# Fewer copies of the features in memory, reads cut in halves and in kinds, and attention's last period rearranged

## The reference, cut to what matters

```python
x = x + attn_a(layernorm(x), Wq, Wk, Wv, Wo)
x = x + ffn(layernorm(x), gate_cp, up_cp, down_cp)
x = x + attn_b(layernorm(x), Wq, Wk, Wog, Wig, g_weight)
x = x + ffn(layernorm(x), gate_cp, up_cp, down_cp)
```

## Time and profile before

| | us |
|---|---|
| median of 3 runs | 833.07 (832.21 to 833.85) |
| profiled execution, its own time | 834.41 |
| its span | 832.7 |
| PE busy | 772.9 (93%) |
| DVE busy | 625.8 (75%) |
| ACT busy | 493.9 (59%) |
| packets of SP's transfers | 108.47 MB, 49.3% of 16 engines |

### The profile page before, as it was taken

How to read it: one execution, slowest core, us unless ns; L and a number is a source line. 1 busy time by engine, 2 the same in 40 slices (tenths; PEclk the granted TensorE clock), 3 DMA queues, 4 the chain that set the end, 5 groups by cost and what they waited for, 6 DMA issues and landing times.

```text
span 832.7 us, 19301 instructions
## 1 busy us (share of the span) xinstructions
PE 772.9 (93%) x6818; PEld 661.5 (79%) x6818; DVE 625.8 (75%) x1269; ACT 493.9 (59%) x967; POOL 244.1 (29%) x321
## 2 busy tenths in 40 slices
PE   7789999999999999779999989999999879999988
PEld 7667777777777777559989878998888859988887
DVE  5677777777787788557887768689887667777765
ACT  3145555555554556565666656678887746666643
POOL 4056743222223233311100010166566470000000
PEclk9899999999999999869999999999999989999999
DMA  6765557666586456675666630000043135777731
GB/s 166 115 135 88 93 100 114 97 96 93 87 147 99 80 81 98 210 260 206 232 238 238 236 132 2 1 2 0 2 149 142 38 142 194 273 264 262 261 131 52
DMA packets 70983, 111.48 MB, mean 134 GB/s; under 512 B 7061, under 2 KB 27958, under 8 KB 70854
## 3 DMA queue, kind: packets, MB, share of 16 engines
q1 hardware_dynamic: 68848, 108.47, 49.3%
q10 hardware_dynamic: 2048, 1.88, 1.1%
HBM read 41.82 MB, written 42.81 MB: 102 GB/s over the span
## 4 chain that ended last, share of the span: by engine, by line
PE 54%; DVE 12%; DMA 10%; SPq 9%; issue 9%; ACT 6%; ACTq 0%; DVEq 0%; POOL 0%; POOLq 0%
PE bank L417 8%; PE bank L419 7%; PE bank L418 7%; DMA stk<-fx 5%; PE pair_a L923 5%; SPq L607 4%; PE bank L937 3%; PE pair_b L892 3%; DVE inter L1968 3%; DMA fx<-fs 2%; PE pair_a L1228 2%; SPq L490 2%; DVE spline L2046 2%; PE pair_a L1173 2%; ACT gact L1547 2%
## 5 line engine op out<-in xcount | busy, mean ns | idle before, releaser
L417 PE MATMUL bank<-wd_hi,in_hi 128*128 128x256 f32 x512 | 147.0, 287 | 0.9 <-DVE in_lo L1973 0.8
L419 PE MATMUL bank<-wd_hi,in_lo 128*128 128x256 f32 x512 | 146.1, 285 | 0.0
L418 PE MATMUL bank<-wd_lo,in_hi 128*128 128x256 f32 x512 | 145.9, 285 | 0.0
L1790 DVE TENSOR_REDUCE mx<-pair_b 128x6 f32<-128x768 f32 x124 | 117.9, 951 | 34.4 <-PE pair_b L904 32.2
L1555 ACT ACTIVATE in_hi<-inter 128x512 fp32r<-128x512 f32 x128 | 80.7, 631 | 105.6 <-DVE inter L1968 101.6
L683 POOL TENSOR_SCALAR_AFFINE_SELECT prob<-prob 128x512 f32<-128x512 f32 x128 | 82.1, 642 | 201.4 <-ACT prob L1390 201.3
L1390 ACT ACTIVATE prob<-pair_a 128x768 f32<-128x768 f32 x128 | 103.6, 810 | 63.0 <-PE pair_a L923 61.2
L1973 DVE TENSOR_TENSOR in_lo<-inter,in_hi 128x512 fp32r<-128x512 f32 x128 | 89.0, 695 | 60.9 <-ACT in_hi L1555 59.4
L417 PEld LDWEIGHTS bank<-wd_hi,in_hi 128*128 128x128 f32 x512 | 98.3, 192 | 6.2 <-DVE in_lo L1973 1.7
L418 PEld LDWEIGHTS bank<-wd_lo,in_hi 128*128 128x128 f32 x512 | 98.2, 192 | 4.8
L419 PEld LDWEIGHTS bank<-wd_hi,in_lo 128*128 128x128 f32 x512 | 98.1, 192 | 0.0
(11 more groups left out here) (233 smaller groups left out, 1960.3 us busy)
## 6 DMA issues: line engine op xcount, KB each, us to landing
stk<-fx SPq DMA_DIRECT2D x128, 252.0 KB
stack<-stage SPq DMA_DIRECT2D x184, 128.0 KB, 4.4
fx<-fs SPq DMA_DIRECT2D x32, 512.0 KB, 3.6
fx<-fs SPq DMA_DIRECT2D x32, 256.0 KB, 3.8
fx<-fs SPq DMA_DIRECT2D x16, 504.0 KB
fx<-fs SPq DMA_DIRECT2D x16, 252.0 KB
X<-in_attn_a_x SPq DMA_DIRECT2D x14, 256.0 KB, 5.4
result<-X SPq DMA_DIRECT2D x7, 512.0 KB, 8.0
```

The costliest lines, as they stand in the source:

```text
L417: pe.matmul(dst, l_hi, r_hi, start=first, stop=False)
L418: pe.matmul(dst, l_hi, r_lo, start=False, stop=False)
L419: return pe.matmul(dst, l_lo, r_hi, start=False, stop=last)
L1790: dve.tensor_reduce(mx[:, h, :, p % PR, :], src[:, :, 0:3 * P].rearrange("p n (t k) -> p n t k", t=3), AX.X, ALU.max).then_inc(a_mx, 1)
```

## The change

Fewer copies: `fx` has two copies instead of three; the third group of reads takes the high copy again. A slot is written by one transfer.

Split reads: a pair is read in two halves (m 0 to 3, m 4 to 7) with semaphores of their own, and each block in two transfers: six groups to partitions 0 to 83, three groups to partitions 84 to 125. The first half of pair g+2 is issued at the end of SP's period g, the second half of g+1 at the start of period g.

Attention: the features of pair 0 are written earlier in period 14, its reads and the writes of pairs 1 and 2 stand inside period 15. The down rows are read in periods 10 to 12 by ACT's queue and split in periods 13 and 14. The third normalisation moves from ACT to DVE; the transpose and high parts of pair 2 from step 7 to step 6; a silu of one column after the last exponential; `keep_clock(8)` at seven places on PE. In the feed-forward `normalise4` is spread over m 4 and 5.

```diff
-        fx = nc.dram_tensor("fx", [2, 3 * FROWS + P, 2 * S], F32, kind="Internal").ap()
+        fx = nc.dram_tensor("fx", [2, 2 * FROWS + P, 2 * S], F32, kind="Internal").ap()
...
-            def load_down(groups):
-                sp.wait_ge(s_wdx, 32)
...
                 if nxt and not nxt2:
-                    load_down(range(KG // 2))
+                    f1_write_x(0, 0)
                 if nxt:
                     max_rows(b + 1, 1 - u, 0)
...
+                if not nxt:
+                    sp.wait_ge(s_zeros, 32)
+                    sp.wait_ge(a_stp, upto(a_stp, B - 2, NP))
+                    f1_read(0, 0, 0)
+                    f1_write_x(1, 1)
+                    f1_read(0, 0, 1)
+                    f1_write_moments(1, 1)
+                    f1_write_x(2, 0)
...
                 def write(u, slot, at, n, landed):
-                    sp.dma_start(copies[u, 0:2, at:at + n, :].rearrange("v p t -> p v t"),
+                    sp.dma_start(copies[u, :, at:at + n, :].rearrange("v p t -> p v t"),
                                  fs[0:n, :, slot, :].bitcast(F32)).then_inc(landed, 16)
-                    sp.dma_start(copies[u, 2, at:at + n, :], fs[0:n, 0, slot, :].bitcast(F32)).then_inc(landed, 16)
...
-                def read(g, u):
-                    sp.wait_ge(f_.xw, upto(f_.xw, base + g, 64))
-                    sp.wait_ge(f_.mw, upto(f_.mw, base + g, 32))
-                    sp.wait_ge(f_.upp, upto(f_.upp, base + g - 1, 1))
-                    for m in range(MT):
+                def read(g, u, half):
+                    sp.wait_ge(f_.xw, upto(f_.xw, base + g, 32))
+                    sp.wait_ge(f_.mw, upto(f_.mw, base + g, 16))
+                    sp.sem_inc(passed_sp, 1)
+                    sp.wait_ge(f_.upp, upto(f_.upp, base + g - 2, MT // 2 * (half + 1)))
+                    for m in range(MT // 2 * half, MT // 2 * (half + 1)):
                         at = 2 + KG * m
-                        rows = fx[u, at:at + 9 * FSTEP, :].rearrange("(r q) t -> r q t", q=FSTEP)[:, 0:NB, :]
-                        sp.dma_start(stk[0:NFX, u, m, :].bitcast(F32), rows).then_inc(f_.ld, 16)
+                        for to, kinds in ((0, 6), (2 * NF, 3)):
+                            rows = fx[u, at:at + kinds * FSTEP, :].rearrange("(r q) t -> r q t", q=FSTEP)[:, 0:NB, :]
+                            sp.dma_start(stk[to:to + kinds * NB, u, m, :].bitcast(F32), rows
+                                         ).then_inc(f_.ld[u][half], 16)
 
                 def period(g, u, prev=True, nxt=True, nxt2=True, nxt3=True):
                     if nxt2 and prev:
                         write_x(g + 2, u)
-                    if nxt:
-                        read(g + 1, 1 - u)
+                    if nxt and prev:
+                        read(g + 1, 1 - u, 1)
                     if prev:
                         store(g - 1)
                     else:
                         first()
                     if nxt2:
                         write_moments(g + 2, u)
+                        read(g + 2, u, 0)
...
             sp.wait_ge(a_stp, upto(a_stp, B - 1, NP))
+            for half in range(2):
+                f1_read(1, 1, half)
             run_f1(sp)
...
+                        if p < 6 and p != 1:
+                            keep_clock(8, bank_p)
...
+                    if b in (10, 11, 12) and p in (2, 6, 7):
+                        first = 6 * (b - 10) + 2 * (2, 6, 7).index(p)
+                        load_down(range(first, min(first + 2, KG)))
...
-                        if p == 4:
-                            f1_normalise(2)
-                        if p in (2, 4, 6, 7):
-                            high_down((p - 1) // 2)
...
-                        if m == 5 and nxt3:
-                            normalise4(g + 3)
+                        if m in (4, 5) and nxt3:
+                            normalise4(g + 3, range(TB * (m - 4), TB * (m - 3)))
...
+                        if p == 2:
+                            third_normalised()
```

More of the change, by code:

```diff
@@ L194, in build @@
         wd_lo = sb("wd_lo", [P, MT, D], F32R)
+        silu_first = sb("silu_first", [P, 1], F32)
         mom = sb("mom", [P, CT, MT * KG], F32)
@@ L364, in ffn_semaphores @@
             f.pe = [f.xT, f.mp, f.gp, f.upp, f.dp]
-            f.xw, f.mw, f.ld = own("xw", 64), own("mw", 32), own("ld", 16 * MT)
-            f.sp = [f.xw, f.mw, f.ld]
+            f.xw, f.mw = own("xw", 32), own("mw", 16)
+            f.ld = [[own(f"ld{u}{half}", 8 * MT) for half in range(2)] for u in range(2)]
+            f.sp = [f.xw, f.mw] + f.ld[0] + f.ld[1]
             return f
@@ L646, in _ @@
             f2_write_moments(0, 0)
-            f2_read(0, 0)
+            for half in range(2):
+                f2_read(0, 0, half)
             f2_write_x(1, 1)
             f2_write_moments(1, 1)
+            for half in range(2):
+                f2_read(1, 1, half)
             f2_write_x(2, 0)
@@ L745, in period @@
                         f1_rstd(1)
-                    if p == 2 and not nxt:
+                    if p == 1 and not nxt:
                         f1_rstd(2)
@@ L1320, in last_attention @@
                     turn_o(B - 1, 1)
+                    keep_clock(8, bank_t)
                 if m == 1:
                     turn_att(B - 1)
+                    pe.wait_ge(a_res, upto(a_res, B - 2, 1))
+                    keep_clock(8, bank_p)
                 if m == 2:
@@ L1434, in spread_rows, with load_down @@
                     act.activation(wdn[:, 0, :, 0:1], wdn[:, 0, :, D:D + 1], ACT.Copy).then_inc(s_wdn, 1)
+            def load_down(groups):
+                act.wait_ge(s_wdx, 32)
+                for k in groups:
+                    act.dma_start(wd_lo[8 * k:8 * k + 8, :, :].bitcast(F32),
+                                  wdx[64 * k + 1:64 * k + 65].rearrange("(m j) d -> j m d", j=8)).then_inc(s_wd, 16)
             def high_down(n):
@@ L1493, in period @@
                             f1_high_moments(0, bank_p)
-                        if p == 6:
-                            f1_normalise(1)
+                        if p in (6, 7):
+                            f1_normalise(1, range(TB * (p - 6), TB * (p - 5)))
                     if not nxt:
-                        if p in (1, 7):
+                        if p == 7:
+                            act.activation(silu_first[:, :], quarter[:, :], ACT.Silu)
+                        if p in (1, 6):
                             for c in range(CT):
@@ L1529, in normalise4 @@
                     act.sem_inc(passed_act, 1)
-                    for t in range(2 * TB):
+                    for t in tiles:
                         act.activation(xr[:, t, :], X[:, bass.ds(2 * TB * g + t, 1), :], ACT.Identity,
@@ L1922, in period, with third_normalised @@
                             f1_stats(2)
-                        if p in (2, 4, 6, 7):
-                            low_down((p - 1) // 2)
+                    if b == B - 3 and p in (6, 7):
+                        low_down(p - 6)
+                    if b == B - 2 and p in (0, 6):
+                        low_down(2 + p // 6)
             attention = period
+            def third_normalised():
+                dve.wait_ge(f_.mr, upto(f_.mr, 2, 1))
+                dve.wait_ge(f_.xT, upto(f_.xT, 1, CT))
+                for t in range(2 * TB):
+                    dve.tensor_scalar(xr[:, t, :], X[:, 4 * TB + t, :], frs[:, t:t + 1], fnmr[:, t:t + 1],
+                                      ALU.mult, ALU.add).then_inc(f_.xn, 1)
             def low_down(n):
```

32 lines of the change are left out of this document (18 added, 14 removed).

## The result

The changed kernel takes **922.59 us** (916.24 to 925.81) beside 832.64 us (831.65 to 833.85) of the kernel before on the same chip: ratio 1.107, 95% interval 1.100 to 1.114. Slower, as predicted, and inside the range of 875 to 935. The forecast of 904 was 18.6 us too low, and the experiments show where from.

The account below looks back on a forecast made before the run. PE bounded the feed-forward before; after, the busiest DMA engines would. 834.4 + 36.9 (first feed-forward) + 34.0 (second) = 905.3 us for the profiled execution, less 1.3 to the median: 904 us, range 875 to 935.

Parts of the forecast that it names:

- The engine sets: Feed-forward reads of `stk`: transfers of 6 and 3 groups get 6 and 3 engines, the 3 among the 6.
- The load of the busiest engine: Feed-forward pair: 274 rows on the busiest engine instead of 187, 23.8 us, over PE's 18.9; 25.8 with the pause between reads.
- The bubble: Feed-forward, before each pair's first half read: 1.5 us from issue to data plus 0.5 us to see the landing.
- the 87 foretold: DMA transfers: price of a 2 KB row on one engine, 87 ns, from 213 GB/s over nine engines; bounds 83 and 97.
- First feed-forward: First read issued at 345.9, last half pair landed at 545.8, block 7 starts at 552.1 instead of 515.2: +36.9 us.
- the down rows on ACT's queue: Attention: 16 issues at 0.36 us, two at a time behind an exponential; hidden, at most 1 us in all if not.
- Second feed-forward: Pairs 0 and 1 read during GLA for nothing; block 7 at 856.0 instead of 822.0: +34.0 us.
- The small edits: Attention and feed-forward: waits vanish or are covered, splits 0 to 1 us, `keep_clock(8)` 0, at most 0.5 us each.
- near 357: Attention's end: time at which PE would be ready for pair 0, instead of 365.75.
- rival (a): Feed-forward reads: 3-engine transfers run on other engines than the 6, PE stays the bound, 808 us; chance 0.10.
- (b): Feed-forward: clock stays at 1.2 GHz after gaps of 3 us twice a pair, 1060 us; chance 0.03.
- (c): Feed-forward: each small transfer costs its engines a fixed 0.3 us, 5 us a pair, 966 us; chance 0.03.

Follow-up runs that it names:

- the order of 14: Reads' source with the 14 rows of a group, not the groups, as outer count: changed kernel 843.09 us; kernel before 827.63 us.
- the feed-forward part alone: Kernel before with two copies, reads in halves and in groups of 6 and 3, normalise4 over two blocks, attention as before: 908.58 us, ratio 1.0904.
- the kernel with the down rows' edit alone: Kernel before with 14 outer rows in its reads, plus down rows read by ACT's queue in periods 10 to 12: 843.57 us, ratio 1.0158.

## Why the prediction was right, and where it was off

**The engine sets: right.** The step was drawn from shares of 9, 14 and 16 engines for a case with 6 and 3 that no row showed. The shares of 0.38 and 0.19 to 0.20 are those sizes, and the 3 do lie inside the 6: while transfers of both sizes are in flight the share stays at 0.38. The landings say the same: the traces also record when each engine's share of a transfer has landed, and a read has 9 landings in the kernel before, 14 with the order of 14, and the eight transfers of a half read of the changed kernel have 36, four times 6 and four times 3. Changing the order of the source's dimensions, and nothing else that counts, takes the loss away.

**The load of the busiest engine: right.** Foretold were 25.8 us a pair, measured 25.6, in the second feed-forward 27.3 (25.8 and 1.5 for the stores) beside 26.0 to 27.3. The bubble was 2.0 us, as foretold (512 to 514). The 23.6 us left of 25.6 are 86 ns for each of the 274 rows (an estimate that takes the busiest engine to be never idle outside the bubble), beside the 87 foretold. One price is a simplification: from 506 to 512, with three engines at 76 GB/s, a row takes 81 ns, below the lowest bound of 83; from 498 to 502, with six at 139 GB/s, 88 ns.

**First feed-forward: the length right, the start wrong.** From the issue of the first read to the last block's gate matmul 206.2 us were foretold (345.9 to 552.1) and 205.2 measured (360.27 to 565.43). The read was issued 14.4 us later than foretold. This is the step that failed: "the down rows on ACT's queue ... hidden, at most 1 us in all if not", measured at 14.9 and 15.9 us. The step priced what the issue costs ACT, and that price held (0.27 to 0.47 us where 0.36 was taken). It did not ask who waits for what shares the DMA engines with those rows: the max rows of the next batch, which PE gets 2.4 us after their last issue and for which it already stood 0.8 us at 252.28 before the change. An engine that waits at once for a small transfer has no slack to give. Waits for max rows grow from 1.1 us to 10.6 us in periods 10 to 12, and the granted clock falls to 0.50 behind the longer ones, which is the likely remainder (last section).

**Second feed-forward: right, 2 us too much.** Foretold +34.0 us, measured +31.9 with GLA between. No wait in its first two pairs, as said.

**The small edits.** PE would be ready for pair 0 "near 357": in the kernel that has all of the change but the down rows and the group sizes it began at 361.7, 4.1 us before instead of 8.8. The kernel before with the order of 14 alone begins at 365.1, and yet the second feed-forward's last gate matmul stands at 815.2 in it and at 815.4 in this one, so none of that lead reaches the end. That these gains lie beside the DMA chain was right for the changed kernel: without the 14.9 us of the down rows it would stand at 907.7, and the feed-forward part alone took 908.6. But that they would be worth 25.5 us without the chain, as rival (a) had it, was wrong: with 14 engines the time is 828.2, not 808. In that kernel the first pairs of each feed-forward take 16.9 to 19.4 us and the last three of the first 19.0 to 20.8, the last two of the second 20.8 and 20.9: what is won early is lost late. In the second feed-forward this is again a wait of PE for reads of `stk`, 5.6 us from 758 to 816. What makes those reads late, SP's issuing of 16 transfers a pair or the wait for the writes ahead of them, was not tested.

**The rivals.** (a) fell with the shares. (b), the clock at 1.2 GHz, fell: the mean clock of the span is 0.94, and after PE's wait of 5 us it is 0.50 from 499.5 to 502.9 and then back at 1.00. (c), a fixed time per small transfer, fell: with twice the transfers and 14 engines pairs take 17.5 us.

**The total.** 916.24 less 834.4 is 81.8: 50.2 for the first feed-forward and what stands before it (foretold 36.9), 31.9 for GLA and the second (34.0), −0.3 behind it. So the profiled execution missed by 13.3 − 2.1 − 0.3 = +10.9 us, and the median lies 6.3 us above this execution, which was the fastest of the four; the 1.3 us by which the profiled execution before stood over its median, which the forecast took off, make up the 18.6.

## What to carry to other kernels

Before a transfer is cut into parts, look at the outermost count of both sides and at the DMA share of the old one: a share that stands at k sixteenths says how many engines carry it, and a cut from 9 groups into 6 and 3 put twice the rows of a read on the busiest engines here, while the order of two dimensions gave the 79.5 us back. Price a transfer that is moved under a busy stretch not by its issue, nor by mean DMA share, but by the smallest transfer there that an engine waits for at once. And a gain at the start of a stage is counted only after asking which wait takes its place later in that stage.

## What the runs showed of the hardware that was not expected

**Few down rows delay the max rows by more than their bytes.** 16 transfers of 64 KB, moved two at a time, cost 15 us in sum; over eight engines at 23.7 GB/s each (the rate behind the prediction's 87 ns) they are 5.5 us, an estimate. What they delay is the landing. In periods 10 to 12 of the kernel before, the last landing of a batch of four max rows comes 1.1 to 2.4 us after their last issue, and in the changed kernel 5.1, 3.6, 1.7, 3.5, 1.5 and 3.2 us, 9.8 us more in sum; in all but one of these six PE's next matmul starts 0.04 or 0.05 us after it. For the first batch the trace has both parts: the last packet on SP's queue ahead of the landings starts at 252.08, not at 250.64, and from there to the last landing (254.97, and 252.23 before) pass 2.9 instead of 1.6 us.

The stretches in which PE stands, of the changed kernel and of the kernel with the down rows' edit alone (columns as above):

```profile
252.00:253.00 1.00, 0.00 (x0) 0.00 (x0) 1.00 (x2) 0.16 (x1) 0.00 (x0) 1.00 0.07 9
```

```profile
251.00:252.00 1.00, 0.00 (x0) 0.00 (x0) 0.82 (x2) 0.00 (x0) 0.00 (x0) 1.00 0.05 8
```

Nearly all that is moved in them is one packet of 8 KB on the queue that the profile calls instruction (4.6% of the 16 engines' time in each), so PE waits while hardly any data moves. It is not one engine that works off the max rows: a batch of four has 16 landings, four for each, so four engines carry a max row, and a transfer of down rows has eight. Queue (ACT's or SP's) and moment were varied, and neither alone takes the loss away: the same order of issue at 275.7 to 276.3 costs PE only 0.16 us, and rows placed behind the max rows still cost. Why the landings come late stays open.

**A wait for max rows costs more than itself.** In the changed kernel PE stands from 251.5 to 255.0, with a granted clock of 1.00 at first. One stretch of it:

```profile
254.00:255.00 1.00, 0.00 (x0) 0.00 (x0) 0.00 (x0) 0.00 (x0) 0.00 (x0) 0.50 0.66 193
```

The granted clock is 0.50, that is 1.2 GHz, here and up to 260, when PE has been at work again for five microseconds; at half the clock these lose 2.5 us beside the 3.5 of the wait. Of the 14.8 us by which periods 10 to 12 grow, 9.5 are longer waits (10.6 less 1.1), and this is the likely rest.
